# Norm sums of the QK projection: four 32-column selections against one 128-column selection that adds up in a bank

## The chip, the cores and the metric

The kernel runs on one NeuronCore of a Trainium2 chip. The metric is the device time of one execution in microseconds (us). The engines are called PE (TensorE; PEld is its weight load), DVE (VectorE), ACT (ScalarE), POOL (GpSimd) and SP (the queue that issues the DMAs).

## The reference, cut to what matters

One transformer layer on x of 4096 x 512 (float32): 16 heads of 32, a LayerNorm over all 512 elements of q and of k, causal attention, a residual and a norm, then a gated feed-forward of width 2048 with dequantised integer weights, a residual and a norm.

```python
qkv = jnp.einsum('bsd,de->bse', x, Wqkv)
q, k, v = jnp.split(qkv, 3, axis=-1)
q = _layernorm_scale_only(q, q_ln_scale)
k = _layernorm_scale_only(k, k_ln_scale)
scores = jnp.einsum('bshd,bthd->bhst', q / jnp.sqrt(jnp.float32(HEAD_DIM)), k)
```

The change touches something the reference does not have. The kernel exponentiates scores without subtracting a row maximum, and that is safe only while the scores are bounded. So while it projects, it computes for every head and token the squared length of q and of k, keeps the largest, and sets a flag if their product is above a bound. The flag chooses between the plain attention and one with a shift.

## The kernel before, in words

Three parts follow one another: `project` (q, k, v), `attend` and `finish` (output projection and feed-forward). Only `project` changes. It works in eight chunks of 512 tokens. A chunk has 12 **units** (four token tiles times q, k, v). A unit is 12 matmuls on PE (L281, 128x128 stationary, 512 columns, type float32r: hi and lo parts of x and of the weights) that add up in one of four banks `acc`.

DVE and POOL normalise each q and k tile (L454 to L463 and L250). When a chunk's eight tiles are normalised, the next chunk's units carry eight **jobs** for it (L89 to L93, one in each of units 2 to 9; the last chunk does its predecessor's jobs in units 1 to 7 and its own in its last four units, two in each). A job `i` stands for q (0 to 3) or k (4 to 7) and a group of 128 of the 512 elements, that is, four heads:

- PE transposes four 128x128 tiles into the bank `turn` (L303).
- ACT squares them into `squares`, bf16 (L373), and scales and rounds them into `part_hi` (L374). Before squaring it waits until norm matmul i-2 has read the buffer that it overwrites (L371).
- DVE makes `part_lo` (L448), and SP stores both parts.
- PE's **norm matmul** (L312) multiplies `squares` with `select`, which adds up the 32 squares of each head. It runs two jobs late, right behind the transposes of a later job, from the list `due` (L318 to L340). In the units after the last job it stands between two units.

`select` is 128x32: column h (0 to 3) holds ones in the rows of head h, the other 28 columns are zero. Group g of q or k writes rows 32g to 32g+31 of the bank `norms_q` or `norms_k`, each norm matmul on its own. After the fourth, DVE takes the largest value of each row (`top`, L469), and the first norm matmul of the next four waits for that (L310). At the end DVE, PE and DVE again make the flag (L503 to L512, L349). SP reads it at the start of `attend` and then loads q, k and v back.

At the start DVE writes the constants, `select` among them (L411 to L419), before it makes the low parts of the first x and weights (L423, L431), for which PE waits. PE waits for `dconst` 3, that is, for `select`, before anything else.

Of the kernel before, what the change touches and what calls it, by code (L numbers as in the profile page):

```python
# [32 lines left out]
BF16 = mybir.dt.bfloat16  # L33
# [5 lines left out]
P = 128  # L39
# [3 lines left out]
HD = D // HEADS  # L43
# [4 lines left out]
DC = D // P  # L48
HG = P // HD
# [11 lines left out]
def over_chunks(engine, body):  # L61


    body(0, -1, 0, False, True, 0)
    with engine.Fori(0, NCH // 2 - 1) as i:
        body(i * 2 + 1, i * 2, 1, True, True, i)
        body(i * 2 + 2, i * 2 + 1, 0, True, True, i + 1)
    body(NCH - 1, NCH - 2, 1, True, False, NCH // 2 - 1)


def project(nc, io, dr, keep):
# [12 lines left out]
    def plan(before, after):  # L84

        units = usual if after else final
        jobs = [[] for _ in units]
        if before:
            for i in range(NJ):  # L89
                jobs[2 + i if after else 1 + i * 6 // (NJ - 1)].append((False, i))  # L90
        if not after:
            for i in range(NJ):
                jobs[8 + i // 2].append((True, i))  # L93
        return list(zip(units, jobs))

    with ExitStack() as c:
        sb = lambda n, s, d=F32: c.enter_context(nc.sbuf_tensor(n, s, d))
# [10 lines left out]
        squares = sb("squares", [P, 2, CH], BF16)  # L108
# [1 line left out]
        ow_hi, ow_lo = keep["ow_hi"], keep["ow_lo"]  # L110
        v_out = sb("v_out", [P, 2, D])
        ident = sb("ident", [P, P])
        select = sb("select", [P, HD], BF16)
        stats = sb("stats", [P, 6])
        mv = sb("mv", [P, 2, 2])
        veps = sb("veps", [P, 2])
# [18 lines left out]
        norms = [c.enter_context(nc.psum_tensor(f"norms_{n}", [P, 512], F32)) for n in "qk"]  # L135
# [22 lines left out]
        norms_done = sem("norms_done")  # L158
# [101 lines left out]
        @block.tensor  # L260
        def _(pe):
            pe.sem_inc(high_done, 2)
            pe.sem_inc(low_done, 2)

            def wait_bank(n, c, units, u):

                if u < ACCS:
                    if isinstance(n, int) and n == 0:
                        return
                    n, (st, m) = c, usual[u - ACCS]  # L270
                else:
                    st, m = units[u - ACCS]
                if m == 2:
                    pe.wait_ge(v_taken, ST * n + st + 1)
                else:
                    pe.wait_ge(qk_normed, 2 * ST * n + 2 * st + m + 1)

            def product(bank, par, st, m, dc):
                rows = slice(st * P, (st + 1) * P)
                for a, (x, w) in enumerate(((x_hi, w_hi), (x_hi, w_lo), (x_lo, w_hi))):  # L280
                    ins = pe.matmul(bank[:], x[:, par, dc, rows], w[:, dc, m * D:(m + 1) * D],  # L281
                                    start=dc == 0 and a == 0, stop=dc == DC - 1 and a == 2)
                return ins

            def unit(n, c, par, units, u):
                st, m = units[u]
                wait_bank(n, c, units, u)
                if u == 0:

                    pe.wait_ge(x_low, DC * n + DC)  # L290
                for dc in range(DC):
                    ins = product(acc[u % ACCS], par, st, m, dc)
                ins.then_inc(acc_full, 1)

            def job(o, par, i):

                pe.wait_ge(high_done, NJ * o + i + 1)
                pe.wait_ge(low_done, NJ * o + i + 1)

                pe.wait_ge(qk_normed, 2 * ST * o + 2 * ST)  # L300
                for st in range(ST):
                    g = i % DC
                    ins = pe.transpose(turn[i % 2][:, st * P:(st + 1) * P], normed[:, par, i // DC, st, g * P:(g + 1) * P], ident[:])  # L303
                ins.then_inc(turned, 1)

            def norm(o, i):

                pe.wait_ge(sq_ready, NJ * o + i + 1)
                if i % DC == 0:
                    pe.wait_ge(norms_read, 2 * o + i // DC + 1)  # L310
                g = i % DC
                pe.matmul(norms[i // DC][g * HD:(g + 1) * HD, :], select[:], squares[:, i % 2, :],  # L312
                          start=True, stop=True).then_inc(norms_done, 1)

            def body(n, c, par, before, after, half):
                steps = plan(before, after)
                units = [x for x, _ in steps]
                due = []  # L318
                for u, (_, jobs) in enumerate(steps):
                    if before or u >= 3:  # L320
                        unit(n, c, par, units, u)
                    elif u == 0:

                        for dc in range(DC):
                            pe.wait_ge(x_low, dc + 1)
                            for m in range(3):
                                pe.wait_ge(w_low_done, 3 * dc + m + 1)
                                ins = product(acc[m], par, 0, m, dc)
                                if dc == DC - 1:
                                    ins.then_inc(acc_full, 1)  # L330
                    for own, i in jobs:
                        o = n if own else c
                        job(o, par if own else 1 - par, i)
                        if len(due) > 1:
                            norm(*due.pop(0))
                        due.append((o, i))
                    if not jobs and due:
                        norm(*due.pop(0))
                while due:
                    norm(*due.pop(0))  # L340

            pe.wait_ge(ident_ready, 1)
            pe.wait_ge(dconst, 3)
            over_chunks(pe, body)

            pe.wait_ge(high_done, NJ * NCH + 2)
            pe.wait_ge(low_done, NJ * NCH + 2)
            pe.wait_ge(fin, 2)
            pe.transpose(turn[0][0:1, 0:P], check[:], ident[:]).then_inc(check_turned, 1)  # L349
# [60 lines left out]
        def _(dve):  # L410
# [3 lines left out]
            dve.memset(zeros[:], 0.0).then_inc(dconst, 1)  # L414
            dve.memset(select[:], 0.0).then_inc(dconst, 1)
            dve.wait_ge(dconst, 2)
            for h in range(HG):
                ins = dve.memset(select[h * HD:(h + 1) * HD, h:h + 1], 1.0)
            ins.then_inc(dconst, 1)  # L419

            def low_x(n, par, dc):
# [1012 lines left out]
def build(nc, io):  # L1434

    def scratch(name, shape, dt):
        return nc.dram_tensor(name, shape, dt, kind="Internal").ap()

    dr = {
        "q_hi": scratch("q_hi", (D, S), F32), "q_lo": scratch("q_lo", (D, S), F32),  # L1440
        "k_hi": scratch("k_hi", (D, S), F32), "k_lo": scratch("k_lo", (D, S), F32),
        "v": scratch("v_rows", (S, D), F32),
        "shift": scratch("shift", (2, HEADS, S), F32),
        "ctx": scratch("ctx", (D, S), F32),
        "sums": scratch("sums", (NCH, HEADS, CH), F32),
        "inverse": scratch("inverse", (NCH, HEADS, CH), F32),
        "wq": scratch("wq_float", (3 * IC, P, D), F32),
    }
    with ExitStack() as c:
        sb = lambda n, s, d: c.enter_context(nc.sbuf_tensor(n, s, d))  # L1450
        sem = lambda n: c.enter_context(nc.semaphore(n))


        keep = {
            "flags": sb("flags", [P, 2], I32), "ow_hi": sb("ow_hi", [P, NG, D], F32R), "ow_lo": sb("ow_lo", [P, NG, D], F32R),
            "whole": sb("whole", [P, D], F32),
            "parts_stored": [sem(f"parts_stored{i}") for i in range(4)], "v_stored": [sem(f"v_stored{i}") for i in range(2)],
            "wq_stored": [sem(f"wq_stored{b}") for b in range(2)],
            "zero_stored": sem("zero_stored"), "ctx_stored": [sem(f"ctx_stored{b}") for b in range(2)],
        }  # L1460
        project(nc, io, dr, keep)
        attend(nc, io, dr, keep)
        finish(nc, io, dr, keep)
# [30 lines left out]
```

## Time and profile before

| | us |
|---|---|
| three runs, median (lowest, highest) | 2451.99 (2450.62, 2453.79) |
| the profiled execution, its own time | 2452.69 |
| its span in the trace | 2450.9 |
| projection, about | 0 to 340 |
| attention, about | 345 to 1608 |
| last part, about | 1608 to 2451 |

Times in the trace count from the span's start. A row of the timeline gives start, duration, engine, line and tile. The duration of a matmul is modelled to the end of its pipeline, so matmuls in a row overlap in the record. What one costs is the distance from one start to the next. Forms such as 128\*32 are the stationary tile: 128 rows, 32 columns.

### The profile page before, as it was taken

Reading aid. Unit: us, or ns where it says so; the run is one execution under the profiler, and the core shown is the slowest. Engines: PE = TensorE matmul, PEld = TensorE weight load, DVE = VectorE, ACT = ScalarE, POOL = GpSimd, SP = SyncE. Lnnn points to the kernel's source line nnn. Section 1 sums busy time; section 2 is a strip of 40 time slices with the busy share of each in tenths; the row PEclk is TensorE's granted clock in tenths of the full one; section 3 lists DMA queues with packets and bytes.
Section 4 is the critical chain, followed back from the end, with each engine's and each line's share of the span. In section 5 each row is a group of like instructions: output and inputs, shape, how many; then the busy total and the mean of one; then the engine's idle time right before and its main releaser. Section 6 shows DMA issues by size and latency. Waiting matters only on the chain. (4 is left out here: it accounts for less than half of the span.)

```text
span 2450.9 us, 34384 instructions
## 1 busy us (share of the span) xinstructions
PE 2353.8 (96%) x12546; PEld 1404.8 (57%) x12546; DVE 1787.0 (73%) x1821; ACT 1317.0 (54%) x1631; POOL 266.3 (11%) x266
## 2 busy tenths in 40 slices
PE   8999966999999999999999999959999999999997
PEld 7777742333343333443334433338888888888885
DVE  7666664898988989889898898954555565565654
ACT  4444435888888888888888888811111111111111
POOL 1111111210122001221012110100000000000000
PEclk9999977999999999999999999979999999999999
DMA  7766677010550106401064010072021121110100
GB/s 246 244 222 241 215 217 143 23 32 5 107 115 23 32 5 114 108 23 32 6 117 105 23 32 5 5 265 78 18 69 35 36 64 32 44 50 21 35 18 17
DMA packets 126399, 197.36 MB, mean 81 GB/s; under 512 B 14992, under 2 KB 39568, under 8 KB 126224
## 3 DMA queue, kind: packets, MB, share of 16 engines
q1 hardware_dynamic: 126224, 195.10, 28.5%
q8 instruction: 101, 1.65, 0.3%
q14 instruction: 74, 0.61, 0.1%
HBM read 122.70 MB, written 72.35 MB: 80 GB/s over the span
## 5 line engine op out<-in xcount | busy, mean ns | idle before, releaser
L883 ACT ACTIVATE probs<-score 128x1024 f32<-128x1024 f32 (+3 forms) x1152 | 1025.2, 956 | 212.2 <-PE score L801 188.2
L949 DVE TENSOR_TENSOR total<-total,probs 128x2048 f32<-128x2048 f32 (+3 forms) x472 | 983.2, 2083 | 78.5 <-POOL probs L762 35.7
L801 PE MATMUL score<-qstk,kstk 98*128 98x512 f32 (+3 forms) x2304 | 659.4, 408 | 35.4 <-DMA qstk<-shift 18.6
L801 PEld LDWEIGHTS score<-qstk,kstk 98*128 98x128 f32 x2304 | 378.9, 190 | 527.3 <-ACT probs L883 411.1
L817 PE MATMUL ctx_acc<-probs,values 128*32 128x512 f32 (+3 forms) x4608 | 576.7, 573 | 8.3 <-POOL probs L762 8.3
L1288 ACT ACTIVATE hidden<-slot,gate_scale_sb 128x512 f32<-128x512 f32 x128 | 88.3, 690 | 624.9 <-PE slot L1217 624.9
L762 POOL TENSOR_SCALAR_AFFINE_SELECT probs<-probs 128x512 f32<-128x512 f32 x128 | 188.1, 1470 | 1037.2 <-ACT probs L883 1037.2
L1373 DVE SCALAR_TENSOR_TENSOR hidden<-slot,up_scale_sb,hidden 128x512 f32<-128x512 f32 x128 | 96.0, 750 | 262.4 <-ACT hidden L1288 257.7
L817 PEld LDWEIGHTS ctx_acc<-probs,values 128*32 128x32 f32 x4608 | 92.0, 108 | 202.4 <-issue 163.0
L1217 PE MATMUL slot<-xt_hi,wg_sb 128*128 128x512 f32 x512 | 201.8, 394 | 5.2 <-issue 5.2
L1228 PE MATMUL y<-wd_sb,h_hi 128*128 128x512 f32 x512 | 199.4, 389 | 1.4 <-DVE h_lo L1381 1.4
L1217 PE MATMUL slot<-xt_lo,wg_sb 128*128 128x512 f32 x512 | 200.2, 391 | 0.0
L1217 PE MATMUL slot<-xt_hi,wu_sb 128*128 128x512 f32 x512 | 199.9, 390 | 0.0
L1217 PE MATMUL slot<-xt_lo,wu_sb 128*128 128x512 f32 x512 | 199.8, 390 | 0.0
L1228 PE MATMUL y<-wd_sb,h_lo 128*128 128x512 f32 x512 | 199.3, 389 | 0.0
L281 PE MATMUL acc<-w_hi,x_hi 128*128 128x512 f32 x384 | 159.1, 414 | 6.7 <-DVE w_lo L431 6.7
L281 PE MATMUL acc<-w_hi,x_lo 128*128 128x512 f32 x384 | 151.4, 394 | 0.0
L281 PE MATMUL acc<-w_lo,x_hi 128*128 128x512 f32 x384 | 151.3, 394 | 0.0
L954 DVE TENSOR_TENSOR total<-probs 128x2048 f32<-128x2048 f32 (+1 forms) x32 | 71.2, 2225 | 80.6 <-ACT probs L883 79.5
L1159 POOL TENSOR_TENSOR rstd<-veps,minus_half 128x1 f32<-128x1 f32 x64 | 36.8, 575 | 804.5 <-DVE veps L1337 804.5
L1217 PEld LDWEIGHTS slot<-xt_hi,wg_sb 128*128 128x128 f32 x512 | 96.7, 189 | 25.7 <-issue 5.5
L1228 PEld LDWEIGHTS y<-wd_sb,h_hi 128*128 128x128 f32 x512 | 96.1, 188 | 22.1 <-DVE h_lo L1381 2.2
(101 smaller groups left out, 1984.4 us busy)
## 6 DMA issues: line engine op xcount, KB each, us to landing
qstk<-q_hi SPq DMA_DIRECT2D x64, 256.0 KB
kstk<-k_hi SPq DMA_DIRECT2D x64, 256.0 KB, 9.4
wq_int<-in_wq SPq DMA_DIRECT2D x48, 256.0 KB, 3.0
wq_float<-wq_f SPq DMA_DIRECT2D x48, 256.0 KB, 2.7
x_raw<-in_x_t SPq DMA_DIRECT2D x32, 256.0 KB, 3.6
v_rows<-v_out SPq DMA_DIRECT2D x32, 256.0 KB, 2.1
q_hi<-part_hi SPq DMA_DIRECT2D x32, 256.0 KB, 2.1
q_lo<-part_lo SPq DMA_DIRECT2D x32, 256.0 KB, 2.5
```

What stands on the lines that cost most here:

```text
L281: ins = pe.matmul(bank[:], x[:, par, dc, rows], w[:, dc, m * D:(m + 1) * D], start=dc == 0 and a == 0, stop=dc == DC - 1 and a == 2)
L762: pool.affine_select(out=view, in_=view, compare_op=ALU.is_ge, fill=0.0, base=0, pattern=[[0, HG], [1, P]], channel_multiplier=-1).then_in ...
L801: ins = pe.matmul(score[u % RING][:, i, cut(t):], kstk[0:ROWS, h, kb * P:(kb + 1) * P], qstk[0:ROWS, q_buffer[ch], h, cut(t):], start=True ...
L817: ins = pe.matmul(ctx[h * HD:(h + 1) * HD, n0:], values[:, kb, h * HD:(h + 1) * HD], probs[:, t % PB, h, n0:], start=t in first, stop=t in ...
L883: act.activation(probs[:, t % PB, 2 * p:2 * p + 2, cut(t):], score[u % RING][:, :, cut(t):], ACT.Exp).then_inc(exped, 1)
L949: dve.tensor_tensor(into, into, now, ALU.add).then_inc(added, 1)
L954: dve.tensor_tensor(into, probs[:, (t - 1) % PB, :, cut(t):], now, ALU.add).then_inc(added, 2)
L1159: pool.tensor_tensor(rstd[:, k, st:st + 1], veps[:, k, st:st + 1], minus_half[:], ALU.pow).then_inc(rooted[k], 1)
L1217: ins = pe.matmul(slot[pos % 2][q][:], v(w[:, i, dc * P:(dc + 1) * P]), v(x[:, par, dc, :]), start=dc == 0 and a == 0, stop=dc == DC - 1 a ...
L1228: ins = pe.matmul(y[st][:], v(x[:, i % 2, st * P:(st + 1) * P]), v(wd[:, i, :]), start=i == 0 and a == 0, stop=i == IC - 1 and a == 1)
L1288: act.activation(hidden[:, i % 2, :], slot[pos % 2][0][:], ACT.Silu, scale=gate_scale[:, i:i + 1]).then_inc(gated, 1)
L1373: dve.scalar_tensor_tensor(hid, slot[pos % 2][1][:], up_scale[:, i:i + 1], hid, ALU.mult, ALU.mult)\
```

## The change

`select` gets four versions of 128 columns, one for each group g, with the ones in columns 32g to 32g+3. A norm matmul writes all 128 rows of its bank, with zeros added outside its own group, and the four of q (or of k) are one sum: the first starts it, the last stops it. The numbers in the bank, the order of the instructions and all waits are the same. DVE writes 16 small pieces of ones instead of four, and a constant of 128x512 bf16 instead of 128x32.

```diff
-        select = sb("select", [P, HD], BF16)
+        select = sb("select", [P, DC, P], BF16)
...
                 g = i % DC
-                pe.matmul(norms[i // DC][g * HD:(g + 1) * HD, :], select[:], squares[:, i % 2, :],
-                          start=True, stop=True).then_inc(norms_done, 1)
+                pe.matmul(norms[i // DC][:], select[:, g, :], squares[:, i % 2, :],
+                          start=g == 0, stop=g == DC - 1).then_inc(norms_done, 1)
...
-            for h in range(HG):
-                ins = dve.memset(select[h * HD:(h + 1) * HD, h:h + 1], 1.0)
+            for g in range(DC):
+                for h in range(HG):
+                    ins = dve.memset(select[h * HD:(h + 1) * HD, g, g * HD + h:g * HD + h + 1], 1.0)
             ins.then_inc(dconst, 1)
```

## Rows read from the trace of the kernel before

**Rows 1.** The page: busy time of the engines, and PE's granted clock in 40 slices.

```profile
PE 2353.8 (96%) x12546; PEld 1404.8 (57%) x12546; DVE 1787.0 (73%) x1821; ACT 1317.0 (54%) x1631; POOL 266.3 (11%) x266
...
PEclk9999977999999999999999999979999999999999
```

**Rows 2.** Windows: length; PE, PEld, DVE, ACT, POOL busy; clock; DMA share; GB/s.

```profile
98.00:138.00 40.00, 40.00 (x182) 30.28 (x181) 26.80 (x52) 17.64 (x30) 4.34 (x8) 1.00 0.67 232
...
356.00:365.00 9.00, 8.40 (x32) 4.68 (x32) 5.36 (x5) 5.05 (x8) 3.52 (x4) 0.50 1.09 203
...
400.00:420.00 20.00, 16.94 (x92) 7.37 (x92) 7.47 (x4) 11.28 (x15) 3.58 (x3) 0.71 0.25 66
```

**Rows 3.** Waits from 57.4 to 332 us: total us, times, longest.

```profile
ACT squares L373 <- PE norms_q L312: 40.7, 30, 2.5
DVE stats L454 <- PE acc L281: 40.6, 46, 2.2
...
PE turn L303 <- DVE normed_qk L463: 0.6, 1, 0.6
```

**Rows 4.** Timeline, PE and PEld, a job without a norm matmul.

```profile
91.25 0.60 PE L303 MATMUL turn<-ident,normed_qk 128*128 128x128 f32 x4
91.61 0.48 PE L281 MATMUL acc<-w_hi,x_hi 128*128 128x512 f32 x1
91.92 0.40 PE L281 MATMUL acc<-w_lo,x_hi 128*128 128x512 f32 x1
...
91.03 0.58 PEld L303 LDWEIGHTS turn<-ident,normed_qk 128*128 128x128 f32 x4
```

**Rows 5.** Timeline, PE and PEld, a job with a norm matmul.

```profile
97.66 0.60 PE L303 MATMUL turn<-ident,normed_qk 128*128 128x128 f32 x4
98.19 0.39 PE L312 MATMUL norms_q<-squares,select 128*32 128x512 bf16 x1
98.51 0.50 PE L281 MATMUL acc<-w_hi,x_hi 128*128 128x512 f32 x1
98.85 0.40 PE L281 MATMUL acc<-w_lo,x_hi 128*128 128x512 f32 x1
...
98.51 0.19 PEld L281 LDWEIGHTS acc<-w_hi,x_hi 128*128 128x128 f32 x1 [0.23 <-issue]
```

**Rows 6.** Timeline, PE, a norm matmul between two units without a job.

```profile
117.48 0.39 PE L281 MATMUL acc<-w_lo,x_hi 128*128 128x512 f32 x1
...
119.77 0.39 PE L281 MATMUL acc<-w_hi,x_lo 128*128 128x512 f32 x1
120.09 0.39 PE L312 MATMUL norms_k<-squares,select 128*32 128x512 bf16 x1
...
120.74 0.40 PE L281 MATMUL acc<-w_lo,x_hi 128*128 128x512 f32 x1
```

**Rows 7.** Timeline of the attention, PE: last score matmul, first value matmul.

```profile
900.94 0.40 PE L801 MATMUL score<-qstk,kstk 98*128 98x512 f32 x1
...
901.26 0.64 PE L817 MATMUL ctx_acc<-probs,values 128*32 128x512 f32 x4
```

**Rows 8.** Groups by form, 0 to 400 us: count, busy us, mean ns, idle before.

```profile
L281 PEld LDWEIGHTS acc<-w_hi,x_hi 128*128 128x128 f32 x384 | 72.6, 189 | 33.3 <-issue 18.6 <-ACT v_out L379 1.4
...
L312 PEld LDWEIGHTS norms_q<-squares,select 128*32 128x32 bf16 x32 | 3.0, 92 | 5.4 <-issue 5.4
```

**Rows 9.** Timeline, PE: two waits in the projection's last 22 us.

```profile
319.15 0.63 PE L303 MATMUL turn<-ident,normed_qk 128*128 128x128 f32 x4 [0.64 <-DVE normed_qk L463]
...
335.95 0.39 PE L312 MATMUL norms_k<-squares,select 128*32 128x512 bf16 x1 [0.77 <-ACT squares L373]
```

**Rows 10.** Timeline, DVE, start of the kernel.

```profile
2.65 0.35 DVE L418 MEMSET select<- 32x1 bf16 x4
5.18 0.69 DVE L423 TENSOR_TENSOR x_lo<-x_raw,x_hi 128x512 fp32r<-128x512 f32 x1 [2.17 <-ACT x_hi L355]
```

**Rows 11.** Timeline, PE, the attention's longest wait near its start.

```profile
403.06 2.07 PE L801 MATMUL score<-qstk,kstk 98*128 98x512 f32 x4 [18.64 <-DMA qstk<-shift]
```

## The prediction

> **What bounds the kernel now.** I read the page first: PE is busy 96% of the span, and its clock is at the full level but for two places [rows 1]. That share mixes three parts, and only the projection changes, so the second view is the windows of the projection. From 98 to 138 us PE is busy for all 40.00 us at full clock, DVE for 26.80, ACT for 17.64, and the DMA engines for 0.67 of the time [rows 2]. A modelled busy time does not prove a bound, since matmul records overlap. So the third view is the waits: from 57.4 to 332 us PE waits once, for 0.6 us, while ACT's squaring waits 40.7 us for q's norm matmuls and DVE's statistics wait 40.6 us for products [rows 3]. The others wait for PE. What PE saves here shortens the stage, until another engine catches up.
>
> The fourth view is the distance between starts in PE's timeline. Ten steps of ordinary 512-column matmuls take 117.48 to 119.77 us [rows 6], 0.229 us each. A job without a norm matmul takes 0.67 us from its first transpose to the second product matmul [rows 4]. A job with one takes 97.66 to 98.85, 1.19 us [rows 5]. **One norm matmul costs 0.52 us**, more than twice an ordinary one that streams as many columns. Between two units it is the same: 119.77 to 120.74 is 0.97, where two ordinary steps would be 0.46, so 0.51 [rows 6].
>
> Where do the 0.29 us beyond 0.229 go? PEld shows it. Without a norm, the transposes' weights load 0.22 us before the first of them starts, under the matmul ahead [rows 4]. Behind a norm matmul, the next weights load only when the record of the next matmul starts, after 0.23 us without anything to load [rows 5]. So weights aren't loaded under a norm matmul, and one starts only when what is ahead has run out. Two things differ there at once: the norm uses 32 of the array's columns, and it is bf16 between 4-byte types.
>
> **The change, part by part.**
>
> *The norm matmuls, 64 of them (32 each for q and k).* After the change they have the form 128\*128, as what stands around them. Bounds for the new cost, from the nearest rows: at best 0.229 us less the little that bf16 might stream faster, say 0.215; at worst the 0.52 stays and the wider weight load comes on top. That load took 92 ns at 32 columns and takes 189 ns at 128 columns of the 4-byte type [rows 8], 0.10 us more, so 0.62. I take 0.229, because the record nearest in form, same columns and same split of the array, is the ordinary matmul. The type speaks less: in the code the transposes are plain float32 and the products float32r, and between them (91.61 after four transposes, the second product at 91.92) no pause of the norm's kind is seen [rows 4]. In the attention, a step from the 98\*128 form to the 128\*32 form without bf16 takes 900.94 to 901.26, 0.32 us, against 0.23 inside a group [rows 7], the same as from a product to a norm (119.77 to 120.09) [rows 6]. So a step from wide to narrow costs 0.09 us more without bf16 as well. The gain is 0.52 - 0.229 = 0.29 us for each.
>
> The Trainium skill, TensorEngine Tiling (Array Packing), section Key Properties, says that changing the tiling mode, not just the tile, drains the engine. By that rule the whole 0.29 us belongs to the split and goes. The trace agrees as far as it shows the case [rows 4 to 7], but no row has bf16 in the full form.
>
> Against the change speaks the weight load. The Trainium skill, TensorE: Matmul & The Clock Gate, section LDWEIGHTS, has it go by columns, columns / 1.2 ns, which makes 27 ns into 107 ns; if nothing hid the 80 ns, the gain would be an estimated 0.21 us each, 12.5 us in all. The same page's Fast Weight Load, for 128 columns of a type other than float32, would take that back.
>
> *How many lie on the path.* All but the last few. Those of the last two jobs, and the one between their transposes (three), run when PE waits for ACT: the last one starts after 0.77 us of waiting for its squares [rows 9], and behind them follows only the chain ACT, DVE, flag. One stands ahead of the wait at 319.15, where PE waits 0.64 us for the last normalised tile [rows 9]. That tile comes through ACT's and DVE's work on the job before, which starts with PE's transposes and not with how soon PE is through. PE would arrive 0.3 us sooner and wait as much longer, and only about 0.1 us is gained. That leaves 60: 60 x 0.29 = **17.4 us**, and I take off 0.2 for small waits that appear, 17.2 us.
>
> *Who has room.* A chunk takes about 144 x 0.229 + 8 x 0.44 + 8 x 0.52 = 40.7 us now (0.44 is the 0.67 of a plain job less one step) and would take 8 x 0.29 = 2.3 less. DVE's share goes from 0.67 to 0.71, ACT's from 0.44 to 0.47, the DMA's from 0.67 to 0.71 [rows 2]. None becomes the bound over a chunk. ACT's wait ahead of squaring is for norm i-2, which comes right behind the transposes; it starts at most 0.1 us sooner, so ACT's wait of 40.7 us [rows 3] shrinks with the shorter unit. The semaphores and the order of every queue stay, and no DMA is added or moved.
>
> *The accumulation.* The bank is written in 128 rows instead of 32 and added to. The product matmuls do both at 0.229 us [rows 6], so this costs nothing more. DVE reads the bank after the fourth as before.
>
> *The constants on DVE.* Four pieces take 0.35 us [rows 10], near 0.1 from start to start, so 12 more are 1.2 us, and the larger zero fill adds some 0.2. DVE ends 1.4 us later, at about 4.4 us, and is next needed at 5.18, after 2.17 us of waiting for ACT [rows 10]. Cost: nothing. The cover is ACT's first conversion; were it gone, PE's start would be 1.4 us later.
>
> *Behind the projection.* The stores are issued as the parts are made, the flag hangs on the last jobs, and SP issues the attention's loads only behind the flag, so they move up whole. The first long wait, 18.64 us until 403.06, is for one of those loads [rows 11] and moves with them. The clock can disturb this a little. PE runs from 356 to 365 us at 0.50, the 1.2 GHz level, behind its idle time, and again partly in 400 to 420 at 0.71 [rows 2]. If the rise comes sooner or later after the shift, I expect up to 2 us either way; the mean is nothing.
>
> **The sum.** The profiled execution took 2452.69 us, 0.70 above the median of three and 1.8 above its span. Less 17.2 it is 2435.5; against the median, 2434.8. I predict 2434.8.
>
> **The rivals.**
>
> *Forecast, the split was the cost.* 2434.8, own range 2431 to 2440 (0.31 us x 61 = 18.9 on one side, 0.25 x 58 = 14.5 on the other, with 2 us for the clock). Chance 0.76.
>
> *Half of it stays.* The type change, or a wider weight load that isn't covered, keeps one of the two pauses, about 0.15 us. 60 x 0.15 = 9 us, 2443. For it: before each norm 0.09 us are lost, and behind it a whole weight load is exposed (98.51 to 98.85 is 0.34 instead of 0.23) [rows 5], so the two sides may have separate causes. Against it: the exposed load looks the same as behind any narrow form. Chance 0.12.
>
> *The change removes nothing.* If PE pauses between bf16 and the 4-byte types, the narrow form was never the cause, and the time stays within 1 us of 2452. For it: bf16 is the only such type on PE, so no row separates it. Against it: the same step without bf16 [rows 7]. Chance 0.07.
>
> *The other side: the pauses stay and the load grows.* Same mechanism, and the 128-column load (0.10 us more than the 32-column one [rows 8]) stands in the open for each norm, since weights aren't loaded under a neighbour of the other type. 60 x 0.10 = 6 us, 2458. It decides from the point where the pause depends on type alone and the load isn't shortened for bf16; a third of it covered, and it falls within no change. Chance 0.05.
>
> **How the numbers follow.** A difference of 0.2%, 4.9 us, is about what a measurement of this kernel can tell. Faster by more: the forecast and the half case, 0.88. Within: 0.07. Slower: 0.05. The range of 8 in 10 holds the forecast's own range and the half case with its spread, 2430.5 to 2446; outside are the two last cases, 0.12, and some tails.
>
> **What would show it right or wrong.** Right: from turn to the second product matmul with a norm about 0.90 us instead of 1.19; weight loads of the next matmul start under the norm; the last norm matmul near 318.7 instead of 335.95 [rows 9]; a chunk of about 38.4 us. PE's wait near 319 grows to some 0.9 us. The memsets of `select` end before the first low part of x, which stays at 5.18 [rows 10]. Wrong: the step behind the norm still shows 0.32 and 0.34 us with no load under it (type, not split); a weight load of `select` of 0.19 us just ahead of each norm (the load in the open); or the gain is there at the last norm matmul and gone at the wait that ended at 403.06 (a transfer that did not move up) [rows 11].

## The result and the profile after

| | before | after |
|---|---|---|
| median of four runs, us (lowest, highest) | 2451.30 (2450.46, 2453.79) | 2433.96 (2433.10, 2437.91) |
| the profiled execution's span, us | 2450.9 | 2431.4 |

The ratio is 0.993, with a 95% interval of 0.9915 to 0.9946: 17.3 us less. The forecast was 2434.8 us, 17.2 less.

I read the views again in the order of the prediction. First PE's timeline at a job with a norm matmul, to be set against [rows 5]:

```profile
95.33 0.60 PE L303 MATMUL turn<-ident,normed_qk 128*128 128x128 f32 x4
95.77 0.38 PE L312 MATMUL norms_q<-squares,select 128*128 128x512 bf16 x1
95.80 0.58 PE L281 MATMUL acc<-w_hi,x_hi 128*128 128x512 f32 x1
96.22 0.40 PE L281 MATMUL acc<-w_lo,x_hi 128*128 128x512 f32 x1
```

From the first transpose to the second product matmul it is 0.89 us instead of 1.19. Take off the 0.67 of a job without a norm matmul [rows 4], and **a norm matmul costs 0.22 us instead of 0.52**. Mind the third row: the record of the product matmul starts 0.03 us behind that of the norm matmul and lasts 0.58. It can't have started its columns there, since the norm matmul's own step is 0.22. Distances to the record after it are the ones to trust. Over a whole chunk, from the first transposes of one to those of the next, it is 38.31 us (88.93 to 127.24) instead of 40.76 (91.25 to 132.01): 2.45 us for eight norm matmuls, 0.31 each.

The weight loads of the same place, and the groups by form from 0 to 400 us:

```profile
95.11 0.58 PEld L303 LDWEIGHTS turn<-ident,normed_qk 128*128 128x128 f32 x4
95.66 0.10 PEld L312 LDWEIGHTS norms_q<-squares,select 128*128 128x128 bf16 x1
95.77 0.19 PEld L281 LDWEIGHTS acc<-w_hi,x_hi 128*128 128x128 f32 x1
95.99 0.19 PEld L281 LDWEIGHTS acc<-w_lo,x_hi 128*128 128x128 f32 x1
```

```profile
L312 PEld LDWEIGHTS norms_q<-squares,select 128*128 128x128 bf16 x32 | 3.1, 98 | 0.0
...
L312 PEld LDWEIGHTS norms_k<-squares,select 128*128 128x128 bf16 x32 | 3.1, 97 | 4.8 <-issue 3.1 <-ACT squares L373 1.7
```

The selection's load starts before the norm matmul. Before, PEld sat idle for 0.17 us ahead of it and for 0.23 us behind it, the second shown in [rows 5], the first here:

```profile
98.19 0.09 PEld L312 LDWEIGHTS norms_q<-squares,select 128*32 128x32 bf16 x1 [0.17 <-issue]
```

Both are gone. Four times the columns load in 97 to 98 ns instead of 92 [rows 8].

Then the waits of the projection, 57.4 to 315 us, and its end in PE's timeline, with the waits in brackets:

```profile
ACT squares L373 <- PE norms_q L312: 33.6, 22, 2.2
DVE stats L455 <- PE acc L281: 32.9, 32, 2.0
...
PE turn L303 <- DVE normed_qk L464: 0.9, 1, 0.9
```

```profile
302.89 0.63 PE L303 MATMUL turn<-ident,normed_qk 128*128 128x128 f32 x4 [0.86 <-DVE normed_qk L464]
...
317.96 0.39 PE L312 MATMUL norms_k<-squares,select 128*128 128x512 bf16 x1 [0.77 <-ACT squares L373]
...
384.83 2.07 PE L802 MATMUL score<-qstk,kstk 98*128 98x512 f32 x4 [21.49 <-DMA qstk<-shift]
```

The others still wait for PE, only less [rows 3]. The last norm matmul starts 17.99 us sooner (335.95 [rows 9]), and the attention's longest wait near its start ends 18.23 us sooner (403.06 [rows 11]). The spans differ by 19.5 us. The 1.3 us between the last two numbers lie in work that did not change; single executions of the changed kernel, in two series, ran from 2431.1 to 2437.9 us.

At the start, DVE in the changed kernel:

```profile
2.58 0.27 DVE L415 MEMSET select<- 128x256 uint32 x1
2.90 1.52 DVE L419 MEMSET select<- 32x1 bf16 x16
5.05 0.69 DVE L424 TENSOR_TENSOR x_lo<-x_raw,x_hi 128x512 fp32r<-128x512 f32 x1 [0.62 <-ACT x_hi L355]
```

The constants end near 4.4 us and DVE still waits 0.62 us for ACT: the cover of [rows 10] held.

### The profile page after: what moved, and what is told of

It reads as the page before. It is cut to its first block and busy times, and to the rows that moved or that the text cites. A ratio compares the mean times of both kernels' runs of the same rounds, so it can differ in the third digit from the quotient of the medians.

```text
span 2431.4 us, 34396 instructions
## 1 busy us (share of the span) xinstructions
PE 2329.9 (96%) x12546; PEld 1405.1 (58%) x12546; DVE 1787.6 (74%) x1833; ACT 1315.8 (54%) x1631; POOL 268.1 (11%) x266
```

## The experiments

The theory: an ordinary full-width step of PE costs 0.22 to 0.23 us, and what was paid beyond it was the **change of form**, from 128 columns of the array to 32 and back, once in each norm matmul. The rivals: a narrow matmul is slow in itself, the type or the weight load costs something, or the gain is one of order. Distances below are again from the first transpose of a job to the second product matmul behind it, 0.67 us without norm matmuls.

**Narrow, twice.** In the kernel before, every norm matmul is issued twice.

```diff
-                pe.matmul(norms[i // DC][g * HD:(g + 1) * HD, :], select[:], squares[:, i % 2, :],
-                          start=True, stop=True).then_inc(norms_done, 1)
+                for again in range(2):
+                    ins = pe.matmul(norms[i // DC][g * HD:(g + 1) * HD, :], select[:], squares[:, i % 2, :],
+                                    start=True, stop=True)
+                ins.then_inc(norms_done, 1)
```

> The kernel before, with each norm matmul issued twice in a row (same 128x32 selection, same bank rows, each overwriting). Theory A, the cost is the change of form: the pause of 0.29 us is paid once on the way in and out, the second matmul costs only its columns, about 0.22 us; from the transposes to the second product matmul 1.19 becomes about 1.41 us, and the time is the one of before plus 60 x 0.22 = 13 us, near 2464 us. Theory B, a narrow matmul is slow in itself: each costs 0.52 us, the distance becomes 1.71 us, and the time is near 2451 + 31 = 2482 us.

PE's timeline of this kernel:

```profile
99.97 0.60 PE L303 MATMUL turn<-ident,normed_qk 128*128 128x128 f32 x4
100.50 0.60 PE L313 MATMUL norms_q<-squares,select 128*32 128x512 bf16 x2
101.03 0.50 PE L281 MATMUL acc<-w_hi,x_hi 128*128 128x512 f32 x1
101.37 0.40 PE L281 MATMUL acc<-w_lo,x_hi 128*128 128x512 f32 x1
```

1.40 us: the second narrow matmul adds 0.21, while the first costs 0.52. A second narrow matmul is not slow, the way in and out is. The time was 2462.54 us (ratio 1.0051, 1.0034 to 1.0068), 11.2 us over the kernel before in the same series (2451.31), against 13 expected and 31 by the rival.

**Wide, twice.** In the changed kernel.

```diff
-                pe.matmul(norms[i // DC][:], select[:, g, :], squares[:, i % 2, :],
-                          start=g == 0, stop=g == DC - 1).then_inc(norms_done, 1)
+                for again in range(2):
+                    ins = pe.matmul(norms[i // DC][:], select[:, g, :], squares[:, i % 2, :],
+                                    start=g == 0 and again == 0, stop=g == DC - 1 and again == 1)
+                ins.then_inc(norms_done, 1)
...
-                    ins = dve.memset(select[h * HD:(h + 1) * HD, g, g * HD + h:g * HD + h + 1], 1.0)
+                    ins = dve.memset(select[h * HD:(h + 1) * HD, g, g * HD + h:g * HD + h + 1], 0.5)
```

> The changed kernel, with each norm matmul issued twice in a row (selection of 0.5 instead of 1.0, both added up, so the sums are the same). It prices one wide norm matmul on the path. Theory A: a wide norm matmul costs as much as an ordinary one, 0.22 to 0.23 us, so 0.89 becomes about 1.11 us and the time is 2434 + 60 x 0.22 = 2447 us. Rival: part of the cost of the single one was at its borders (a type change), then the second is much cheaper than the first; or the wide bf16 load shows in the open when two norm matmuls follow each other, then the second costs about 0.32 us and the time is near 2453 us.

```profile
97.06 0.60 PE L303 MATMUL turn<-ident,normed_qk 128*128 128x128 f32 x4
97.50 0.59 PE L313 MATMUL norms_q<-squares,select 128*128 128x512 bf16 x2
97.74 0.58 PE L281 MATMUL acc<-w_hi,x_hi 128*128 128x512 f32 x1
98.16 0.39 PE L281 MATMUL acc<-w_lo,x_hi 128*128 128x512 f32 x1
```

1.10 us: the second costs 0.21, the first 0.22. So no cost shows at the borders of the wide form. The time was 2445.91 us (ratio to before 0.9982, 0.9973 to 0.9992), 12.0 over the changed kernel. Some 60 norm matmuls on the path times 0.21 are 12.6.

**Sixty-four columns.** In the changed kernel two groups share a half of the bank.

```diff
-        select = sb("select", [P, DC, P], BF16)
+        select = sb("select", [P, 2, 2 * HD], BF16)
...
-                pe.matmul(norms[i // DC][:], select[:, g, :], squares[:, i % 2, :],
-                          start=g == 0, stop=g == DC - 1).then_inc(norms_done, 1)
+                pe.matmul(norms[i // DC][g // 2 * 2 * HD:(g // 2 + 1) * 2 * HD, :], select[:, g % 2, :], squares[:, i % 2, :],
+                          start=g % 2 == 0, stop=g % 2 == 1).then_inc(norms_done, 1)
...
-            for g in range(DC):
+            for g in range(2):
```

> The changed kernel with 64-column selections: groups 0 and 1 add up in rows 0 to 63 of the bank, groups 2 and 3 in rows 64 to 127. Theory A, any split of the array costs the change of form: 0.52 us for each norm matmul as before, distance 1.19 us, time 2451 us. Rival, the cost goes with how narrow the form is: about halfway, 1.04 us and 2443 us.

```profile
99.07 0.60 PE L303 MATMUL turn<-ident,normed_qk 128*128 128x128 f32 x4
99.59 0.40 PE L312 MATMUL norms_q<-squares,select 128*64 128x512 bf16 x1
99.93 0.50 PE L281 MATMUL acc<-w_hi,x_hi 128*128 128x512 f32 x1
100.26 0.39 PE L281 MATMUL acc<-w_lo,x_hi 128*128 128x512 f32 x1
```

1.19 us, and 2452.87 us (ratio 1.0008, 0.9999 to 1.0018): the whole gain is gone at 64 columns, and PEld's idle times of 0.17 and 0.23 us are back. For 32 and 64 columns it is a matter of split or not, not of how narrow.

**Wide, float32r.** `squares` and the selection are float32r. Room is made by a strip whose windows are the four selections, and by the zero fill in two DMAs (left out below, with the copies that fill the strip).

```diff
-        squares = sb("squares", [P, 2, CH], BF16)
+        squares = sb("squares", [P, 2, CH], F32R)
...
-        select = sb("select", [P, DC, P], BF16)
...
+        select = sb("select", [P, 7 * HD], F32R)
...
-                pe.matmul(norms[i // DC][:], select[:, g, :], squares[:, i % 2, :],
+                pe.matmul(norms[i // DC][:], select[:, (3 - g) * HD:(7 - g) * HD], squares[:, i % 2, :],
                           start=g == 0, stop=g == DC - 1).then_inc(norms_done, 1)
```

> The changed kernel with squares and selection in float32r, the type of the product matmuls, instead of bf16 (the four selections are windows of one strip of 224 columns, and the zero fill of the shift goes in two DMAs, to make room). Its weight load takes 189 ns instead of 97. Theory A: only the form counts, the longer load lies under the matmul ahead, cost 0.23 us, time within 2 us of the changed kernel, 2434 to 2436 us. Rival: bf16 among 4-byte types still costs something at its borders, then this is faster, up to 0.05 us x 60 = 3 us, 2431 us. Second rival: the load is partly in the open, 0.09 us x 60 = 5.5 us more, 2439.5 us.

```profile
98.09 0.60 PE L305 MATMUL turn<-ident,normed_qk 128*128 128x128 f32 x4
98.44 0.48 PE L314 MATMUL norms_q<-squares,select 128*128 128x512 f32 x1
98.76 0.40 PE L283 MATMUL acc<-w_hi,x_hi 128*128 128x512 f32 x1
99.00 0.39 PE L283 MATMUL acc<-w_lo,x_hi 128*128 128x512 f32 x1
```

0.91 us and 2434.52 us (ratio 0.9926, 0.991 to 0.9943), that of the changed kernel. In the full form the two types differ by 0.02 us, and a load of 190 ns instead of 98 shows in the distance by no more than that. A lone narrow matmul in float32r was not run, so whether the narrow form costs the whole 0.30 us between 4-byte types too is not shown. In the attention of the kernel before, with plain float32, a sign of it is there: PEld sits idle for 0.37 us ahead of the narrow loads, and they start only with their matmuls.

```profile
901.26 0.16 PEld L817 LDWEIGHTS ctx_acc<-probs,values 128*32 128x32 f32 x8 [0.37 <-issue]
```

**Wide, overwriting.** This leaves three of the four groups out of the largest norms.

```diff
-                          start=g == 0, stop=g == DC - 1).then_inc(norms_done, 1)
+                          start=True, stop=True).then_inc(norms_done, 1)
```

> The changed kernel with every wide norm matmul overwriting the whole bank instead of adding to it, which leaves three of the four groups out of the largest norms. Theory: adding up in the bank is free and only the form counts, so 0.89 us from transposes to second product, 2434 us. Rival: adding up costs (the bank is read and written), then this is faster by what one addition costs, 0.02 to 0.05 us x 45 = 1 to 2 us, seen in the distances.

From 109.19 (transposes) to 110.08 (second product matmul) it is 0.89 us, the same as with adding up, and the time was 2434.23 us (ratio 0.9926, 0.991 to 0.9943). Adding up in the bank costs nothing that shows.

**Narrow, four in a row.** If only the change of form costs, it can be paid once for four. There are four buffers of squares, and the semaphore `norms_done`, for which ACT and DVE wait, starts at 4 instead of 2. `due` is emptied behind the next job once it holds four, or in the next unit without a job.

```diff
-        squares = sb("squares", [P, 2, CH], BF16)
+        squares = sb("squares", [P, 4, CH], BF16)
...
-                        if len(due) > 1:
-                            norm(*due.pop(0))
+                        if len(due) == DC:
+                            while due:
+                                norm(*due.pop(0))
                         due.append((o, i))
-                    if not jobs and due:
-                        norm(*due.pop(0))
+                    if not jobs:
+                        while due:
+                            norm(*due.pop(0))
```

> The kernel before, with four buffers of squares and the four narrow norm matmuls of q (or of k) issued in a row, once per four jobs, each to its own 32 columns of the array. Theory A1, narrow matmuls in different columns overlap: four of them cost about 0.29 + 0.23 + 3 x 0.02 = 0.58 us together, against 4 x 0.23 = 0.92 in the changed kernel; with 15 such fours on the path 5 us less than the changed kernel, near 2429 us. Theory A2, they run one after the other: 0.29 + 4 x 0.215 = 1.15 us, 15 x 0.23 = 3.5 us more than the changed kernel, near 2437.5 us. If the pause belongs to each narrow matmul (theory B), 4 x 0.52 = 2.08 us, and nothing changes against before: 2451 us.

PE's timeline, at a job behind which q's four follow:

```profile
101.00 0.60 PE L303 MATMUL turn<-ident,normed_qk 128*128 128x128 f32 x4
101.53 0.40 PE L312 MATMUL norms_q<-squares,select 128*32 128x512 bf16 x4
101.86 0.50 PE L281 MATMUL acc<-w_hi,x_hi 128*128 128x512 f32 x1
102.19 0.40 PE L281 MATMUL acc<-w_lo,x_hi 128*128 128x512 f32 x1
```

1.19 us, the same as with one. The second row holds four matmuls in 0.40 us, where one has a record of 0.39. Unlike the two in the same columns, these narrow matmuls, in different columns of the array, run side by side, and **four cost 0.52 us together**, against 4 x 0.22 = 0.88 for the wide ones. The time was **2426.79 us** (2425.47 to 2428.70; ratio to before 0.9907, 0.989 to 0.9923), 7.2 us under the changed kernel's median. This version beats both: its last norm matmul starts at 312.05 us, against 317.96 in the changed kernel.

**Wide, four in a row.** The same order with the wide selection (windows of a strip), as a control.

> Four buffers of squares and the four norm matmuls issued in a row, as in the variant that ran faster than both kernels, but with the wide 128-column selection that adds up. If that variant gains because narrow matmuls in different columns overlap, wide ones cannot: four cost 4 x 0.22 = 0.88 us, and the time is that of the changed kernel, 2434 us, or up to 1.5 us less from ACT's and DVE's shorter waits. If it gains by the new order alone (fewer places, ACT's waits gone), this one is as fast, 2427 us.

From the transposes at 101.42 to the second product matmul at 102.94 it is 1.52 us, so four cost 0.85. The time was 2431.68 us (2430.39 to 2433.23; ratio 0.9915, 0.9899 to 0.9932), 2.3 under the changed kernel, a little more than the 1.5 expected as the most. The last norm matmul starts at 317.03, 0.9 us sooner than in the changed kernel, and at 312.05 in the narrow variant:

```profile
317.03 0.39 PE L312 MATMUL norms_k<-squares,select 128*128 128x512 bf16 x1 [0.77 <-ACT squares L375]
```

```profile
312.05 0.39 PE L312 MATMUL norms_k<-squares,select 128*32 128x512 bf16 x1 [0.77 <-ACT squares L375]
```

Of the 5.9 us between the narrow four and the changed kernel at this place, 5.0 are the overlap, 15 x (0.85 - 0.52) = 5.0, and 0.9 go with the order. The medians give 7.2, of which 4.9 and 2.3. They say it less sharply: the narrow four ran on another chip than the wide four, the kernel before had a median of 2451.31 us on the one and 2452.53 on the other, and the intervals of the two ratios overlap. What the medians show beyond the 5.9 us is not traced to a cause.

**The changed kernel again**, on the chip of the last group of runs.

> The changed kernel once more, on the same chip as the three others, so that differences of 1 to 3 us can be read against it: 2434 us.

2433.90 us (2431.14 to 2435.92; ratio 0.992, 0.9904 to 0.9937), within 0.1 of its first median. Its fastest run is 2.4 us above the slowest of the four narrow in a row (2428.70), which ran on the other chip.

## Why the prediction was right

**The bound.** PE bounds the projection, before and after: its one wait before the last jobs grew from 0.64 to 0.86 us and stayed the only one.

**The price of a norm matmul.** 0.52 us was read from distances, and the gain of 0.29 was taken by the likeness of form. It measured 0.30 (1.19 to 0.89), as a bf16 step costs 0.21 to 0.22 and not the 0.229 of a product step. The type and the split could not be told apart in the trace of before. The changed kernel's own trace decides it, bf16 in the full form at 0.22, and two variants confirm it: bf16 with 64 columns pays as before, and float32r in the full form, at 0.24, is within 0.02 us of it. The rule of the Trainium skill, TensorEngine Tiling (Array Packing), section Key Properties, is that a change of the tiling mode drains the engine. The trace agrees, with a price of 0.30 us for the way in and out together; that a drain fills this time, the records do not show.

**How many.** 60 were put on the path. The last norm matmul moved by 17.99 us, and 17.99 / 0.30 is 60 (59 with the 2.45 / 8 of a chunk). Of the wait at 319.15, "0.9 us" was expected and 0.86 came, so 0.22 of the 0.30 us that one norm matmul saved ahead of it were lost, and about 0.1 was gained, as the prediction had it.

**Luck.** That the medians differ by 17.3 us and the forecast said 17.2 is luck in the last digits. The interval of the ratio is 13 to 21 us, and the trace shows 18.0 us at the last norm matmul, 0.8 more than forecast: 60 x 0.01, since a norm matmul saved 0.30 and not 0.29, and the 0.2 that was taken off for small waits.

**The weight load.** It was the step with the widest bounds, up to 0.10 us more for each. It is 6 ns longer in bf16 and hidden; at 190 ns in float32r it is hidden too. What kept loads in the open was the form on either side, not their length: 92 ns in the narrow form stood in the open, 190 in the full form did not. The Trainium skill, TensorE: Matmul & The Clock Gate, section LDWEIGHTS, has a load go by its columns. These records don't show it: in bf16, 32 columns took 92 ns and 128 took 98, and at 128 columns float32r took 190 and the plain float32 of the transposes 139. What sets these lengths stays open.

**Behind the projection.** The attention's loads moved up whole (18.2 us). The clock's part can't be told from the scatter: the time from the last norm matmul to the end of that wait was 67.1 us before and 66.9 after, but 64.6 to 70.1 over all kernels here with the same work in it, and 70.1 in the second traced execution of the changed kernel itself.

**What the prediction did not see.** It weighed the narrow form as a cost only. The trace of before already has the other side, in the attention:

```profile
901.26 1.06 PE L817 MATMUL ctx_acc<-probs,values 128*32 128x512 f32 x8
902.26 1.20 PE L801 MATMUL score<-qstk,kstk 98*128 98x512 f32 x4
```

Eight records of narrow matmuls, two for each of the four that the code writes into the four column groups, take 1.00 us from start to start, where eight full-width steps would take 8 x 0.23 = 1.84. So four narrow norm matmuls could share one pause and overlap, and that variant has its last norm matmul 5.9 us sooner than the change itself (7.2 us between the medians). The halves of the pause, in and out, were not separated, and eight in a row, q's and k's, were not tried.

## What to carry to other kernels

Read the cost of a small matmul from the distances between the starts around it, and subtract the same place without it. If a matmul on part of the array's columns stands alone between full ones, either pad it to the full width, which makes it an ordinary step, or collect as many as there are column groups and issue them in a row, which makes them one step and one pause. Widening to half the array bought nothing here. The prices are those of 512-column matmuls.

## What the runs showed of the hardware that was not expected

- Four bf16 matmuls of 32 columns each, in different columns of the array, took no more time than one: 1.19 us with four and 1.19 us with one, each from the transposes to the second product matmul. In the same columns, the second one took 0.21 us more.
- The stretch behind the projection, in which q, k and v are read back, varied with the same loads: from the last norm matmul to the end of the attention's longest wait it was 66.9 and 70.1 us in two executions of the changed kernel, and 64.6 to 70.1 over all kernels here. In a single trace this hides a difference of 2 us; the start of the last norm matmul repeated within 0.03 us in two executions of the changed kernel (317.96 and 317.99).
